# x1 kept in place, a later expert schedule, one program for experts and last stage, and one product moved to GpSimd

## The chip, the cores and the metric

The kernel runs on 1 core of one Trainium2 chip. The metric is the device time of one execution in microseconds, lower is better. Before the change it is 1065.08 us, the median of three runs.

## What is computed

The input is 32 blocks of 256 rows of 128 numbers (8192 rows, fp32). First a recurrent cell runs along each block's rows and its normalised output is added to the input, which gives x1. Then comes a layer with causal attention of 16 heads of 8 dimensions inside each block, a router that picks 2 of 8 experts for each row, the experts (128 to 512 to 128, gelu between), and two more norms.

```python
def reference(x, ...):                       # x: (32, 256, 128)
    x = x + cell(layernorm(x))               # the recurrent cell: x1
    return x + ffn(layernorm(x))

def cell(x):
    i, f, o, z = split(x @ W + b)            # 128 x 512
    i, f = softcap(i + input_bias), -softplus(f)
    # along the rows: m' = max(f + m, i); c = e^(f+m-m') c + e^(i-m') tanh(z); n likewise
    h = sigmoid(o) * c / (n + eps)
    return h / rms(h) * scale

def ffn(x):
    q, k, v = split(x @ w_qkv)               # 16 heads of 8
    o = softmax(causal(q @ k.T / sqrt(8))) @ v
    h = layernorm(x + o @ w_o, g1, b1)
    w = top2(softmax(h @ wg))                # 2 of 8 experts
    moe = sum_e w[e] * (gelu(h @ w1[e] + bb1[e]) @ w2[e] + bb2[e])
    return layernorm(h + moe, g2, b2)
```

## The kernel before

All code is written out engine by engine. Each engine has a function `step(s)` that issues its instructions of that step in a fixed order, and waits on semaphores where it needs another's result. fp32 products that need their precision are made from a high and a low part (`_hi`, `_lo`).

**Cell and attention (0 to about 690 us).** 32 blocks `b` of 256 rows go through a pipeline, one step `s` for each. The cell works in 16 groups `g` of 512 rows, one every second step, some steps ahead of the attention. Its tiles are called `a_...`, those of the attention `b_...`. SP (the queue of SyncE) issues the DMAs of this part, in the order of `step(s)`: in even steps the load of a group of the input into `cell.X` (L491, 256 KB, a ring of NC = 3 groups); the block of x1 into `b_X` (L518, 128 KB); the row of the softmax maxima `b_mt` of block s-3 into row M_ROW = 24 of `c_QK` (L522); the high and low parts of the queries and keys of block s-1 out to DRAM scratch `qk_scr` (L529, L530, L532); in odd steps a group of x1 from `cell.X` to DRAM (L536, 256 KB); a row of zeros into row M_ROW of `c_QK` (L541, 16 KB); and four DMAs that read the queries and keys back from scratch in their new layout into `c_QK` (L547). `c_QK` is a ring of NQ = 3 blocks. Before L541 SP waits until PE has read the block that stood in the buffer. On PE, `maximum(b, u)` makes scores for the row maxima in `b_ps_m`, with a mask product first (L1605 or L1612) and then L1608 or L1615 over all 128 partitions of `c_QK`; since row M_ROW would hold the maxima of an older block there, it is zeroed first. DVE reduces them (L1180), ACT takes the exponentials (L811) of a second set of scores (L1591, L1594) that have the maxima row in them. `rows_stats` (L1340) makes the norm's statistics from `b_X`, `rows_norm` (L852) its normalised rows.

**Experts (about 734 to 997 us).** 71 slots of 256 rows each, sorted by expert, 8 slots to one loop round. PE's order in slot s: twelve products of the up projection (L2028 to L2030) into `e_ps`, the transposes of the rows of slot s+1 (`rows_in`, L2008), the transposes of the output of slot s-1 (`rows_out`, L2015), the eight passes of the down projection of slot s (L2039). ACT applies gelu (L1950) and copies the outcome (L1943), DVE copies the slot's weights (L1965, L1966), makes `e_XW` (L1983), `e_x_lo` (L1970) and `e_Y` (L1991). GpSimd scatters the rows to the DRAM tensor `results` (L1923, two indirect DMAs a slot), first all first choices and then all second choices of the 8192 rows. SP loads `e_X` (L1908, a ring of 8 slots), after the results of the slot 8 back have landed.

**Last stage (about 1002 to 1060 us).** `combine` is a program block of its own, with a barrier of all engines ahead of it. 16 groups of 512 rows: SP loads the two results of each row into `f_G` (L2088, two DMAs of 256 KB a group, ring of four groups), PE adds them into `f_A` (L2131, L2132, ring of three), DVE makes the statistics (L2142, L2148), ACT the root (L2099, L2101), DVE the shift (L2155), ACT the normalised rows `f_Y` (L2115, four a group), DVE multiplies by g2 (L2163) and adds x1 (L2167), ACT's queue stores (L2105).

Of the kernel before, what the change touches and what calls it, by code (L numbers as in the profile page):

```python
# [13 lines left out]
P = 128  # L14
# [92 lines left out]
def cell_memory(nc):  # L107

    cell = Cell()
    with ExitStack() as ctx:  # L110
# [17 lines left out]
        cell.X = sb("a_X", [P, NC, 4, D])  # L128
# [20 lines left out]
        cell.r_rms = sb("a_r_rms", [P, 4])  # L149
    return cell  # L150
# [5 lines left out]
M_ROW = ROWS  # L156
# [3 lines left out]
NB = 5  # L160
NQ = 3
CELL = 12032
NC = 3
NX = 3
# [46 lines left out]
def layers(nc, dram, const, kept):  # L211

    x1_t = dram["x1"].rearrange("(b t p) d -> b p t d", p=P, t=2)
# [6 lines left out]
    with ctx:  # L220
# [21 lines left out]
        zero_row = sb("b_zero", [HEADS, T])  # L242
        X = sb("b_X", [P, NX, 2, D])
# [116 lines left out]
        s_x = [sem(f"b_x{k}") for k in range(NX)]  # L360
# [95 lines left out]

        def stored(engine, g):

            engine.wait_ge(c_out[g % NC], 16 * (g // NC) + 16)

# [15 lines left out]
        WRITES, READS = 3 * 16, 5 * 16  # L476
        BROWS = 2 * E + 4
        FILLED = 3 + 2 * NQ
# [10 lines left out]
        def _(sync):  # L489
# [18 lines left out]
            cell_rows(2)  # L508

            def step(s):  # L510
                if s.base % 2 == 0 and NC <= s.base // 2 + NC < GROUPS:
                    stored(sync, s.base // 2)
                    cell_rows(s.base // 2 + NC)
                if s.exists(B):
                    b, n = s, s.of(NX)
                    need(sync, s_xn, b - (NX - 1))
                    stored(sync, b.base // 2)
                    sync.dma_start(X[:, n], x1_t[bass.ds(b.value(), 1)].rearrange("b p t d -> p (b t) d")).then_inc(s_x[n], 16)  # L518
                if (s - 3).exists(B):
                    b, n = s - 3, (s - 3).of(NQ)  # L520
                    need(sync, s_mtc, b + 1)
                    sync.dma_start(QK[M_ROW:M_ROW + 1, n, 0:NJ].rearrange("o j g n -> o (j g) n").bitcast(fp32), mt[:, :].bitcast(fp32)).then_inc(s_mr[n], 16)  # L522
                if (s - 1).exists(B):

                    b, n = s - 1, (s - 1).of(NQ)
                    need(sync, s_qkhi, b + 1)
                    need(sync, s_qkr[n], b.turn(NQ) * READS)
                    slots = scr[n].rearrange("s p n -> p s n")
                    sync.dma_start(slots[:, 0:4:3], qk_hi[:, :, :].bitcast(fp32)).then_inc(s_qkw[n], 16)  # L529
                    sync.dma_start(slots[:, 1:6:4], qk_hi[:, :, :].bitcast(fp32)).then_inc(s_qkw[n], 16)  # L530
                    need(sync, s_qklo, b + 1)
                    sync.dma_start(slots[:, 2:5:2], qk_lo[:, :, :].bitcast(fp32)).then_inc(s_qkw[n], 16)  # L532
                x = group(s, 4)
                if x.exists(GROUPS):
                    need(sync, c_x1, x + 1)
                    sync.dma_start(out_t[:, 4 * x.base:4 * x.base + 4, :], cell.X[:, x.of(NC)]).then_inc(c_out[x.of(NC)], 16)  # L536
                if (s - 1).exists(B):
                    need(sync, s_s, (b - NQ) * 12 + 12)
                    if b.base < NQ:
                        sync.wait_ge(s_fill, FILLED - 2 * (NQ - 1 - n))  # L540
                    sync.dma_start(QK[M_ROW:M_ROW + 1, n, 0:NJ].rearrange("o j g n -> o (j g) n").bitcast(fp32), zero_row[:, :]).then_inc(s_qkr[n], 16)  # L541
                if (s - 1).exists(B):
                    b, n = s - 1, (s - 1).of(NQ)
                    need(sync, s_qkw[n], b.turn(NQ) * WRITES + WRITES)
                    rows = scr[n].rearrange("(a s) (r j g) n -> j (s r) a (g n)", a=2, g=NG, j=NJ)
                    for j in range(NJ):
                        sync.dma_start(QK[32 * j:32 * j + ROWS, n, j:NJ + 1:NJ - j].rearrange("p a g n -> p a (g n)").bitcast(fp32), rows[j]).then_inc(s_qkr[n], 16)  # L547
# [1689 lines left out]
```

## Times and profile before

| | |
|---|---|
| runs | 1067.49, 1065.08, 1062.44 us |
| profiled execution | 1061.42 us, its span 1059.6 us |
| PE busy | 902.4 us (85%) |
| DVE busy | 849.5 us (80%) |
| ACT busy | 769.8 us (73%) |
| GpSimd busy | 535.0 us (50%) |
| DMA | 114.69 MB, 108 GB/s in the mean |

The span is the time from the first to the last recorded instruction of the profiled execution; 1.8 us of its time lie around it. Times of a row are counted from the span's start. "PE" rows are matmuls, "PEld" their weight loads; "SPq" and "ACTq" are DMA issues by SyncE and ScalarE. A value in square brackets is how long the engine stood idle before the row, and what ended that.

### The profile page before, as it was taken

The numbers are of one execution on the slowest core, as the hardware profiler recorded it, in microseconds if no ns is written. First come the engines' busy times: TensorE is split into PE (matmuls) and PEld (weight loads), VectorE is DVE, ScalarE is ACT, GpSimd is POOL, SyncE is SP. The second block draws the span as 40 slices with busy tenths as digits, with TensorE's granted clock in tenths as the row PEclk, the third lists the DMA queues.
The fourth block names the chain that finished last, engine by engine and source line by source line (L and its number), as shares of the span: only waits on it lengthen the run. The fifth ranks groups of instructions, "written<-read, shape, count | busy, mean of one in ns | idle before, by whom it ended". The sixth has DMA issues, their size and how long they took to land. (4 is left out here: it accounts for less than half of the span.)

```text
span 1059.6 us, 26142 instructions
## 1 busy us (share of the span) xinstructions
PE 902.4 (85%) x6922; PEld 698.3 (66%) x6922; DVE 849.5 (80%) x2533; ACT 769.8 (73%) x1905; POOL 535.0 (50%) x781
## 2 busy tenths in 40 slices
PE   1446899999999999999999998846999999999474
PEld 0234667676766766766676666536999999999421
DVE  4667989999999999998989888673777777777378
ACT  2776799999999999997897766751656656666356
POOL 8000243344356556656577767782555656656400
PEclk9657999999999999998999999965999999999788
DMA  1015543444354454545344556153333332332186
GB/s 52 1 51 130 132 108 108 113 118 111 90 136 118 120 128 118 136 108 124 104 127 126 137 140 160 40 119 102 88 99 86 92 89 85 95 86 67 48 247 190
DMA packets 138118, 114.69 MB, mean 108 GB/s; under 512 B 19459, under 2 KB 126601, under 8 KB 138005
## 3 DMA queue, kind: packets, MB, share of 16 engines
q1 hardware_dynamic: 120916, 92.24, 33.9%
q0 software_dynamic: 8640, 16.93, 5.0%
q10 hardware_dynamic: 8448, 4.20, 1.4%
q8 instruction: 48, 0.79, 0.3%
q14 instruction: 66, 0.53, 0.2%
HBM read 60.60 MB, written 52.58 MB: 107 GB/s over the span
## 5 line engine op out<-in xcount | busy, mean ns | idle before, releaser
L621 POOL TENSOR_SCALAR_AFFINE_SELECT b_PT<-b_PT 128x256 f32<-128x256 f32 (+1 forms) x384 | 191.0, 512 | 207.2 <-ACT b_PT L811 202.1
L1180 DVE TENSOR_REDUCE b_m_neg<-b_ps_m 128x2 f32<-128x512 f32 (+1 forms) x384 | 255.1, 681 | 33.9 <-PE b_ps_m L1615 15.8
L811 ACT ACTIVATE b_PT<-b_ps_s 128x512 f32<-128x512 f32 x384 | 219.6, 598 | 28.3 <-PE b_ps_s L1591 13.9
L1923 POOL DMA_INDIRECT results<-e_Y,e_X x142 | 151.7, 1068 | 121.4 <-DVE e_Y L1991 98.5
L656 POOL DMA_INDIRECT slots<-c_pay,b_pos x128 | 130.3, 1018 | 39.9 <-issue 36.5
L2039 PE MATMUL e_ps_d<-e_h,e_w 128*128 128x256 f32 x568 | 134.5, 380 | 0.0
L1615 PE MATMUL b_ps_m<-c_QK 128*128 128x256 f32 x512 | 123.3, 322 | 0.0
L1594 PE MATMUL b_ps_s<-c_QK 128*128 128x512 f32 x256 | 111.0, 434 | 5.6 <-ACT b_PT L811 5.4
L1950 ACT ACTIVATE e_h<-e_ps,e_w 128x256 f32<-128x256 f32 x284 | 111.3, 480 | 0.8 <-PE e_ps L2030 0.8
L2039 PEld LDWEIGHTS e_ps_d<-e_h,e_w 128*128 128x128 f32 x568 | 102.6, 191 | 11.0
L1943 ACT ACTIVATE e_yt<-e_ps_d,e_w 128x256 f32<-128x256 f32 x71 | 33.7, 475 | 99.2 <-PE e_ps_d L2039 99.2
L1965 DVE CAST e_w<-c_w1s 128x1024 fp32r x71 | 49.4, 696 | 67.6 <-PE e_ps L2030 66.2
L2028 PE MATMUL e_ps<-e_x_hi,e_w 128*128 128x256 f32 x284 | 93.9, 330 | 0.9 <-DVE e_x_lo L1970 0.9
L1608 PE MATMUL b_ps_m<-c_QK 128*128 128x128 f32 x512 | 94.3, 314 | 0.0
L1627 PE MATMUL b_ps_o<-b_PT,b_V 128*32 128x256 f32 x1024 | 82.7, 395 | 1.1 <-POOL b_PT L621 1.1
L1608 PEld LDWEIGHTS b_ps_m<-c_QK 128*128 128x128 f32 x512 | 79.7, 197 | 3.8
L2030 PE MATMUL e_ps<-e_x_hi,e_w 128*128 128x256 f32 x284 | 80.7, 284 | 0.0
L2029 PE MATMUL e_ps<-e_x_lo,e_w 128*128 128x256 f32 x284 | 80.5, 283 | 0.0
L1615 PEld LDWEIGHTS b_ps_m<-c_QK 128*128 128x128 f32 x512 | 79.6, 196 | 0.5
L1612 PE MATMUL b_ps_m<-mask_b,ident_b 128*128 128x256 bf16 x256 | 72.0, 281 | 6.9 <-DVE b_m_neg L1180 6.6
L1605 PE MATMUL b_ps_m<-mask_b,ident_b 128*128 128x512 bf16 x128 | 50.4, 394 | 26.4 <-DMA c_QK<-qk_scr 20.9
L610 POOL TENSOR_TENSOR a_X<-a_Y,a_X 128x512 f32<-128x512 f32 x16 | 20.5, 1281 | 89.1 <-DVE a_Y L1145 89.1
(253 smaller groups left out, 2311.6 us busy)
## 6 DMA issues: line engine op xcount, KB each, us to landing
c_QK<-qk_scr SPq DMA_DIRECT2D x128, 192.0 KB
qk_scr<-b_qk_hi SPq DMA_DIRECT2D x64, 256.0 KB
e_X<-slots SPq DMA_DIRECT2D x71, 130.0 KB, 2.3
qk_scr<-b_qk_lo SPq DMA_DIRECT2D x32, 256.0 KB
f_G<-results SPq DMA_DIRECT2D x32, 256.0 KB, 3.6
a_X<-in_L_attn_x_dram SPq DMA_DIRECT2D x16, 256.0 KB, 6.4
x<-a_X SPq DMA_DIRECT2D x16, 256.0 KB, 2.8
b_X<-x SPq DMA_DIRECT2D x32, 128.0 KB, 5.7
```

Source lines behind the costliest of these rows:

```text
L621: nc.gpsimd.affine_select(out=tri, in_=tri, compare_op=ALU.is_ge, fill=0.0, base=0, pattern=[[0, tri.shape[1]], [1, P]], channel_multiplie ...
L656: nc.gpsimd.indirect_dma_start(dram["slots"][:, :], bass.IndirectOffsetOnAxis(pos[:, q % NPOS, k, i:i + 1], 0), pay[:, r, t, k, :], None). ...
L811: nc.scalar.activation(PT[:, g % 2, q % 3], ps_s[:, q % 2], ACT.Exp, scale=HD ** -0.5).then_inc(s_e, 1)
L1180: nc.vector.tensor_reduce(out, scores, AX.X, ALU.max, negate=True).then_inc(s_red, 1)
L1594: nc.tensor.matmul(ps_s[:, q % 2].rearrange("p (j q) -> p j q", j=2), QK[:, n, NJ, g, 0:P], QK[:, n, 2 * u - 2:2 * u, g, :], start=True, s ...
L1608: done = nc.tensor.matmul(ps_m[:, u % 2, j * P:(j + 1) * P], QK[:, n, j, u, 0:P], QK[:, n, NJ, u, 0:P], start=False, stop=(j == 3), skip_g ...
L1615: done = nc.tensor.matmul(ps_m[:, u % 2, j * T:(j + 1) * T], QK[:, n, 2 * jp + j, g, P:T], QK[:, n, NJ, g, :], start=False, stop=(j == 1), ...
L1627: nc.tensor.matmul(ps_o[32 * j:32 * j + VW, g // 2, :], v_block(n, 0, g, j), PT[:, g % 2, 1 + j // 2, (j % 2) * T:(j % 2 + 1) * T], start= ...
L1923: nc.gpsimd.indirect_dma_start(dram["results"][:, :], bass.IndirectOffsetOnAxis(X[:, j.of(NB_X), u, D:D + 1].bitcast(u32), 0), Y[:, n, u, ...
L1950: nc.scalar.activation(h1[:, n, c], ps_1[:, c, 0:SUB * P], ACT.Gelu_apprx_tanh, bias=w2[:, n, F + c:F + c + 1]).then_inc(s_g, 1)
L2028: nc.tensor.matmul(out, w1[:, n, 1, col], x_hi[:, n], start=True, stop=False)
L2039: last = nc.tensor.matmul(ps_d[:, 0:SUB * P], w2[:, n, c * D:(c + 1) * D], h1[:, n, c], start=(c == 0), stop=(c == NF - 1))
```

## The change

1. The tile `b_X` and its 32 loads are gone. `rows_stats` and `rows_norm` read block b out of `cell.X`, where the cell has left x1. The ring of `cell.X` grows from 3 to 6 groups. The next group is loaded by `recurrent_in` at the end of an even step, when the group six back has been stored and the rows of its second block have been normalised. The load used to stand at the head of an even step, directly behind the reads of the odd step.
2. The maxima row moves from partition 24 to partition 127, and the products for the maxima read partitions 0 to 119 only (KEYS = 120). The row of zeros is no longer written. The wait that stood before it stands before the reads.
3. The results of one row lie side by side in DRAM, and the 64 rows of one partition (row p*64 and after) too: `dest` gives p*128 + 2t + k for row t of partition p and choice k. The last stage loads a group in one DMA of 512 KB with 4 KB pieces, where it took two of 256 KB with pieces of 512 bytes.
4. Experts: in step s PE now does the up projection of s, `rows_in` of s+2, `rows_out` of s-2, and the down projection of s-1. Up projections of even and odd slots go to different halves of `ps_1`, w2 has four buffers in place of two. ACT and DVE follow (`yt` and `Y` of s-2, halves of s+2).
5. `combine` gives back functions that the experts' block calls at its end; there is no block of its own and no barrier between. `f_A` is `ps_1`. SP waits for the last results by itself, PE for the last gelu.
6. The product with g2 goes from DVE (L2163) to GpSimd.

```diff
-NC = 3
-NX = 3
+NC = 6
+KEYS = 32 * (NJ - 1) + ROWS
-M_ROW = ROWS
+M_ROW = 127
+            def recurrent_in(s):
+                g = s.base // 2 - 1 + NC
+                if s.base % 2 or not NC <= g < GROUPS:
+                    return
+                stored(sync, g - NC)
+                need(sync, s_xn, Count(2 * (g - NC) + 2))
+                cell_rows(g)
...
+            def operands(b):
...
+                need(sync, s_qkw[n], b.turn(NQ) * WRITES + WRITES)
+                need(sync, s_s, (b - NQ) * 12 + 12)
...
+                for j in range(NJ):
+                    sync.dma_start(QK[32 * j:32 * j + ROWS, n, j:NJ + 1:NJ - j]..., rows[j]).then_inc(s_qkr[n], 16)
...
             def step(s):
-                if s.base % 2 == 0 and NC <= s.base // 2 + NC < GROUPS:
-                    stored(sync, s.base // 2)
-                    cell_rows(s.base // 2 + NC)
-                if s.exists(B):
-                    b, n = s, s.of(NX)
-                    need(sync, s_xn, b - (NX - 1))
-                    stored(sync, b.base // 2)
-                    sync.dma_start(X[:, n], x1_t[...]).then_inc(s_x[n], 16)
...
-                    sync.dma_start(QK[M_ROW:M_ROW + 1, n, 0:NJ]..., zero_row[:, :]).then_inc(s_qkr[n], 16)
+                a, b1, x = s - 1, s - 3, group(s, 4)
+                maxima_row(b1)
+                columns_high(a)
+                columns_low(a)
+                recurrent_out(x)
+                operands(a)
+                recurrent_in(s)
...
             for s in range(GROUND, STEPS_B):
                 step(Count(s))
+                if s == B - 2:
+                    stored(sync, GROUPS - 1)
...
-                nc.gpsimd.iota(dest[:, :, :], pattern=[[P, NTILE], [B * T, TOPK]], base=0, channel_multiplier=1)
+                nc.gpsimd.iota(dest[:, :, :], pattern=[[TOPK, NTILE], [1, TOPK]], base=0, channel_multiplier=TOPK * NTILE)
...
             def rows_stats(n):
-                need(dve, s_x[k], n.turn(NX) * 16 + 16)
+                need(dve, c_x1, Count(n.base // 2 + 1))
                 need(dve, s_mv, n)
                 for t in range(2):
-                    last = nc.vector.bn_stats(stats[:, t, :], X[:, k, t, :])
+                    last = nc.vector.bn_stats(stats[:, t, :], cell_row(n, t))
...
-                        done = nc.tensor.matmul(ps_m[...], QK[:, n, j, u, 0:P], QK[:, n, NJ, u, 0:P], ...)
+                        done = nc.tensor.matmul(ps_m[...], QK[0:KEYS, n, j, u, 0:P], QK[0:KEYS, n, NJ, u, 0:P], ...)
...
+    r_t = dram["results"].rearrange("(p t k) d -> p t k d", p=P, k=TOPK)
+    def on_sync(sync):
+        for sem_of, count in landed:
+            sync.wait_ge(sem_of, count)
+        for g in range(GROUPS):
...
+            sync.dma_start(G[:, n], r_t[:, 4 * g:4 * g + 4]).then_inc(s_g[n], 16)
...
+    def on_gpsimd(pool):
+        for g in range(GROUPS):
+            m = g % 2
+            pool.wait_ge(s_y0, 4 * g + 4)
+            if g >= 2:
+                pool.wait_ge(s_y3, g - 1)
+            nc.gpsimd.tensor_tensor(Y1[:, m], Y0[:, m], kept["g_b"][:, :, :].to_broadcast([P, 4, D]), ALU.mult).then_inc(s_y1, 1)
...
+        def summed(g):
+            dve.wait_ge(s_y1, g + 1)
...
+            nc.vector.tensor_tensor(Y3[:, g % 3], Y1[:, m], kept["x1"][:, 4 * g:4 * g + 4, :], ALU.add).then_inc(s_y3, 1)
...
             def step(s):                      # PE, experts
...
+                        if c % 2 == 0:
+                            need(pe, s_g, (s - 2) * NF + (c + 2))
...
-                if (s + 1).exists(SLOTS):
-                    rows_in(s + 1)
-                if (s - 1).exists(SLOTS):
-                    rows_out(s - 1)
-                if s.exists(SLOTS):
-                    need(pe, s_yt, s)
+                if (s + 2).exists(SLOTS):
+                    rows_in(s + 2)
+                if (s - 2).exists(SLOTS):
+                    rows_out(s - 2)
+                j = s - 1
+                if j.exists(SLOTS):
+                    need(pe, s_yt, j)
```

The order of the DMAs on SP in an odd step of the pipeline and in the even step behind it, before (lines without an x count are one DMA):

```order
L532 DMA qk_scr<-b_qk_lo 128x2x256
L536 DMA x1<-a_X 128x4x128
L541 DMA c_QK<-b_zero 1x16x256
L547 DMA c_QK<-qk_scr 24x2x1024 x4
L491 DMA a_X<-in_L0_attn_x_dram 128x4x128
L518 DMA b_X<-x1 128x2x128
L522 DMA c_QK<-b_mt 1x16x256
L529 DMA qk_scr<-b_qk_hi 128x2x256
L530 DMA qk_scr<-b_qk_hi 128x2x256
L532 DMA qk_scr<-b_qk_lo 128x2x256
L541 DMA c_QK<-b_zero 1x16x256
L547 DMA c_QK<-qk_scr 24x2x1024 x4
```

and the same stretch now, with the line numbers of the changed kernel:

```order
L544 DMA qk_scr<-b_qk_lo 128x2x256
L550 DMA x1<-a_X 128x4x128
L562 DMA c_QK<-qk_scr 24x2x1024 x4
L525 DMA c_QK<-b_mt 1x16x256
L534 DMA qk_scr<-b_qk_hi 128x2x256
L535 DMA qk_scr<-b_qk_hi 128x2x256
L544 DMA qk_scr<-b_qk_lo 128x2x256
L562 DMA c_QK<-qk_scr 24x2x1024 x4
L491 DMA a_X<-in_L0_attn_x_dram 128x4x128
```

The loads of `a_X` and `b_X` no longer follow the reads of the odd step; that of `a_X` now follows the reads of the even step, and that of `b_X` and the zero row are gone.

PE at the end of the experts, after the last product of the last up projection, before:

```order
L2030 MATMUL e_ps_1<-e_x_hi,e_w1 128x256
L2015 MATMUL e_ps_y<-ident,e_yt 128x128 x2
L2039 MATMUL e_ps_d<-e_h1,e_w2 128x256 x4
L2015 MATMUL e_ps_y<-ident,e_yt 128x128 x2
L1855 UNCONDITIONAL_BRANCH
L2124 UNCONDITIONAL_BRANCH
L2131 MATMUL f_A<-f_G,ident 128x512
```

and now:

```order
L2203 MATMUL e_ps_1<-e_x_hi,e_w1 128x256
L2186 MATMUL e_ps_y<-ident,e_yt 128x128 x2
L2213 MATMUL e_ps_d<-e_h1,e_w2 128x256 x4
L2186 MATMUL e_ps_y<-ident,e_yt 128x128 x2
L2213 MATMUL e_ps_d<-e_h1,e_w2 128x256 x4
L2186 MATMUL e_ps_y<-ident,e_yt 128x128 x2
L1961 MATMUL e_ps_1<-f_G,ident 128x512
```

One more down projection and one more pair of transposes stand behind the last up projection, and the branches to another program are gone.

DVE in two groups of the last stage, before:

```order
L2155 SCALAR_TENSOR_TENSOR f_shift<-f_mv,f_rstd 128x4
L2142 BN_STATS f_st<-f_A 128x6 x4
L2148 BN_AGGR f_mv<-f_st 128x2 x4
L2163 TENSOR_TENSOR f_Y1<-f_Y0,c_g 128x512
L2167 TENSOR_TENSOR f_Y3<-f_Y1,c_x1 128x512
```

and now, where GpSimd has sixteen rows of the product behind its last scatter:

```order
L1984 SCALAR_TENSOR_TENSOR f_shift<-f_mv,f_rstd 128x4
L1971 BN_STATS f_st<-e_ps_1 128x6 x4
L1977 BN_AGGR f_mv<-f_st 128x2 x4
L1992 TENSOR_TENSOR f_Y3<-f_Y1,c_x1 128x512
```

DVE's add now waits for GpSimd, and the next group's statistics stand behind it in the same queue.

## Rows read from the trace of the kernel before

**Rows 1.** Windows: stretch, length, busy of PE PEld DVE ACT POOL, clock, DMA share, GB/s.

```profile
300.00:400.00 100.00, 94.01 (x827) 68.72 (x829) 96.51 (x265) 93.04 (x222) 58.85 (x97) 1.00 0.48 120
...
600.00:690.00 90.00, 80.52 (x762) 55.22 (x761) 70.86 (x230) 61.15 (x149) 64.75 (x115) 0.98 0.44 116
```

**Rows 2.** Waits in 80 to 690 us: engine, line, releaser, total us, times, longest.

```profile
PE b_ps_m L1605 <- DMA c_QK<-qk_scr: 20.9, 18, 3.7
...
SPq L541 <- PE b_ps_s L1594: 63.4, 29, 3.4
...
SPq L547 <- DMA qk_scr<-b_qk_lo: 4.9, 7, 1.7
```

**Rows 3.** Timeline of PE, a block's first product: four of the eighteen waits.

```profile
88.25 0.61 PE L1605 MATMUL b_ps_m<-mask_b,ident_b 128*128 128x512 bf16 x1 [3.74 <-DMA c_QK<-qk_scr]
...
105.70 0.39 PE L1605 MATMUL b_ps_m<-mask_b,ident_b 128*128 128x512 bf16 x1 [1.07 <-DMA c_QK<-qk_scr]
...
341.72 0.39 PE L1605 MATMUL b_ps_m<-mask_b,ident_b 128*128 128x512 bf16 x1 [0.94 <-DMA c_QK<-qk_scr]
...
493.26 0.54 PE L1605 MATMUL b_ps_m<-mask_b,ident_b 128*128 128x512 bf16 x1 [2.09 <-DMA c_QK<-qk_scr]
```

**Rows 4.** Timeline of SP's queue: an early even step, then odd and even step.

```profile
98.66 1.55 SPq L547 DMA_DIRECT2D c_QK<-qk_scr  x4
...
332.78 0.51 SPq L541 DMA_DIRECT2D c_QK<-b_zero  x1
333.66 1.56 SPq L547 DMA_DIRECT2D c_QK<-qk_scr  x4
335.26 0.39 SPq L491 DMA_DIRECT2D a_X<-in_L_attn_x_dram  x1
335.76 0.45 SPq L518 DMA_DIRECT2D b_X<-x  x1
...
351.38 2.10 SPq L547 DMA_DIRECT2D c_QK<-qk_scr  x4
```

**Rows 5.** Window behind the longest wait of the middle.

```profile
494.00:504.00 10.00, 9.79 (x62) 7.03 (x62) 6.23 (x17) 5.78 (x12) 4.24 (x7) 0.69 0.30 96
```

**Rows 6.** Windows: a hundred us of the experts; early in the last stage.

```profile
800.00:900.00 100.00, 100.00 (x669) 94.22 (x668) 73.83 (x224) 61.01 (x168) 59.53 (x57) 1.00 0.32 90
1010.00:1030.00 20.00, 14.63 (x30) 5.27 (x29) 16.64 (x77) 11.90 (x38) 0.00 (x0) 0.95 0.81 232
```

**Rows 7.** Timeline in the experts: a second scatter, then SP's next load.

```profile
861.36 1.03 POOL L1923 DMA_INDIRECT results<-e_Y,e_X  x1 [0.30 <-issue]
...
863.87 0.40 SPq L1908 DMA_DIRECT2D e_X<-slots  x1
```

**Rows 8.** DMA issues of the page: median us from issue to landing.

```profile
slots<-c_pay,b_pos POOLq DMA_INDIRECT x128, 3.4
```

**Rows 9.** Timeline, from the last slot to the last stage's first product.

```profile
992.82 0.44 PE L2015 MATMUL e_ps_y<-ident,e_yt 128*128 128x128 f32 x2 [0.56 <-ACT e_yt L1943]
...
996.08 0.98 POOL L1923 DMA_INDIRECT results<-e_Y,e_X  x1 [0.30 <-issue]
...
1006.24 2.08 PE L2131 MATMUL f_A<-f_G,ident 128*128 128x512 f32 x2 [12.98 <-DMA f_G<-results]
```

**Rows 10.** Chain that ended last: its first load, two turns of its loop.

```profile
1001.62 0.37 SPq L2088
...
1021.74 1.10 PE f_A L2131 x2
1022.83 0.87 PE f_A L2132 x2
...
1027.15 1.10 PE f_A L2131 x2
```

**Rows 11.** One 128x512 product on GpSimd and on DVE, ns min/median/max.

```profile
L610 POOL TENSOR_TENSOR a_X<-a_Y,a_X x16: 1267/1282/1294, 57.0 to 596.1; 128x512 f32<-128x512 f32 x16
...
L2163 DVE TENSOR_TENSOR f_Y<-f_Y,c_g x16: 655/658/693, 1016.2 to 1055.5; 128x512 f32<-128x512 f32 x16
```

More of the change, by code:

```diff
@@ L149, in cell_memory @@
         cell.r_rms = sb("a_r_rms", [P, 4])
+        cell.X = sb("a_X", [P, NC, 4, D])
     return cell
@@ L161 @@
 NQ = 3
-CELL = 12032
-NC = 3
-NX = 3
+CELL = 13056
+NC = 6
 NV = 4
@@ new lines, in _, with maxima_row @@
+            for g in range(3, NC):
+                cell_rows(g)
[5 more added lines that the diff above has]
+                need(sync, s_xn, Count(2 * (g - NC) + 2))
+                cell_rows(g)
+            def maxima_row(b):
+                if not b.exists(B):
+                    return
+                n = b.of(NQ)
+                need(sync, s_mtc, b + 1)
+                sync.dma_start(QK[M_ROW:M_ROW + 1, n, 0:NJ].rearrange("o j g n -> o (j g) n").bitcast(fp32), mt[:, :].bitcast(fp32)).then_inc(s_mr[n], 16)
@@ new lines, in columns_high, with columns_low @@
+            def columns_high(b):
+                if not b.exists(B):
+                    return
+                n = b.of(NQ)
+                need(sync, s_qkhi, b + 1)
+                need(sync, s_qkr[n], b.turn(NQ) * READS)
+                slots = scr[n].rearrange("s p n -> p s n")
+                sync.dma_start(slots[:, 0:4:3], qk_hi[:, :, :].bitcast(fp32)).then_inc(s_qkw[n], 16)
+                sync.dma_start(slots[:, 1:6:4], qk_hi[:, :, :].bitcast(fp32)).then_inc(s_qkw[n], 16)
+            def columns_low(b):
+                if not b.exists(B):
+                    return
+                n = b.of(NQ)
+                need(sync, s_qklo, b + 1)
+                need(sync, s_qkr[n], b.turn(NQ) * READS)
+                slots = scr[n].rearrange("s p n -> p s n")
+                sync.dma_start(slots[:, 2:5:2], qk_lo[:, :, :].bitcast(fp32)).then_inc(s_qkw[n], 16)
@@ L1890, in run_experts @@
         s_go = sem("e_go")
+        last_stage = combine(nc, ctx, dram, const, kept, ps_1,
+                             [(s_out[k], 32 * len(range(k, SLOTS, NB_E))) for k in range(NB_E)], (s_g, SLOTS * NF))
         block = ctx.enter_context(nc.Block())
@@ L1996, in step @@
                     nc.vector.tensor_tensor(row, row, kept["b_b"][:, :, :], ALU.add).then_inc(s_xb, 1)
-            steps(dve, SLOTS, 1, NB_X, step, 8)
+            steps(dve, SLOTS, 2, NB_X, step, 8)
             dve.wait_ge(s_xb, NTILE)
+            last_stage["vector"](dve)
         @block.tensor
@@ L2179, in constants @@
+            steps(pe, SLOTS, 2, NB_X, step, 8)
+            last_stage["tensor"](pe)
 def constants(nc, ctx, dram):
```

339 lines of the change are left out of this document (154 added, 185 removed).

## The prediction

> **What bounds the kernel now.** I read the windows of busy time first, then the table of waits, then the timeline of SP's queue, and the chain of work for the end.
>
> In the pipeline (80 to 690 us) two engines are nearly full: in the middle window PE is busy 94.0 and DVE 96.5 of 100 us [rows 1]. Only in 600 to 690 is DVE free a fifth of the time (70.9 of 90). PE's own greatest wait is for the queries and keys, 20.9 us in 18 waits at the first product of a block [rows 2]. In the middle they come every second step, .2 to 1.2 us each, ten of them 8.8 us in sum with the one of 2.09; the first three (3.74, 1.07, 1.62) make 6.4 and the last five 5.7; four of the eighteen are shown [rows 3]. SP's queue says why every second one: behind the four reads of an odd step stand at once the loads of `a_X` and `b_X`, 384 KB, and those reads need 341.72 - 333.66 = 8.1 us until PE may start. The early even step, with `b_X` alone behind, needs 105.70 - 98.66 = 7.0 [rows 3, 4]. Ahead of the reads the zero row takes .51, and its wait for PE is a long one in 29 of 32 steps [rows 2, 4].
>
> In the experts PE is busy 100.00 of 100 us [rows 6]; nothing but PE's own work counts there, 3.6 us a slot. Between the last slot and the last stage lie a landing, the end of a program and a first load [rows 9, 10]. The last stage is a loop of 1027.15 - 1021.74 = 5.41 us for two groups: PE's sums, DVE's statistics, ACT's root and rows. L2163 isn't in it [rows 10].
>
> **The reads of queries and keys (parts 1 and 2).** Two things bring them earlier. Without the zero row SP issues them up to .55 sooner; where the writes to scratch land last (7 waits of L547 [rows 2]; at 333.66 a gap of .37 [rows 4]) it is nothing, so 0 to .55. With nothing behind them in an odd step they take at most the 7.0 of the step that had `b_X` behind, 1.0 less. Together 1.0 to 1.6, against waits of .2 to 1.2. Of the ten middle waits all but a rest of the 2.09 go: 8 us of PE time. DVE has the same work as before, at 96% busy, and part of the time won waits for it, so I count half: **-4**. At the start the first and third reads have nothing behind them and the second now has `a_X`: about 3 of 6.4 us go, -2.5. At the end DVE isn't full and counts whole, but the last three reads have weight loads behind them that stay; the first two of the five (.8 each) go, and up to .5 from each of the other three where the writes let them: -2. Sum **-8.5**. Bounds: -2 if DVE alone sets the middle; -20 if all 20.9 goes.
>
> In the even steps the load of `a_X` now stands where `b_X` did, 128 KB more. By the 8.1 above the reads come 1.1 later, less the zero row's .55. No even step of the middle shows a wait: the timeline has all ten of them behind an odd step's reads, so there is some room over the 7.0. I take it that it holds .5 and count nothing; if it doesn't, up to .5 in each of 12 even steps (+6). The statistics read `cell.X` itself, so their rows are there a store and a load earlier; the ring of six groups gives the loads twelve steps. One wait for the last store is new, at a point where it was issued a whole step before; behind it stand only weight loads. Partitions 0 to 119 in place of 128 change no count of columns: nothing.
>
> **Experts (part 4).** PE issues the same instructions in a slot and never waits, so a slot stays 3.6 us: 0 in 71 slots. The first up projection now stands behind the transposes of two slots' rows: +.2, a guess. At the end one down projection and one pair of transposes follow that before ran under an up projection: work is only moved, but the stall of .56 at L2015 [rows 9] comes twice and the outcome's last rows one turn later, +.8. Sum **+1**, bounds 0 and +2.5. SP loads slot s+8 2.5 us behind the scatter [rows 7], or 3.4 by the page's row for the other scatter [rows 8]. PE now wants the rows a slot earlier and gives results a slot later; of some 13 us of slack 6 stay.
>
> **One program (part 5).** The last scatter starts at 996.08, so its rows land at 998.6 to 999.5; the first load is issued at 1001.62 [rows 9, 10]. SP now waits for the landing itself: 2.1 to 3.0 go, **-2.6**. If other engines' ends had cost nothing it would be 0. Without the second issue (.37) -.4. The first sum on PE takes 2.08 at a lowered clock where a later one takes 1.10 [rows 9, 10]; PE stands idle there as before, so I count no gain.
>
> **The product on GpSimd (part 6).** Its like on GpSimd takes 1.28 us, on DVE .66 [rows 11]. DVE's busy time falls by 16 x .66 = 10.5, but it isn't in the loop. What is: the add of group g waits for the product, and shift and the statistics of group g+3 stand behind it. From ACT's last row of group g: product 1.28 with handovers .15, add .69, shift .16, so 2.3 us; PE's sum of g+3 is there after .14 + 1.10 + .87 = 2.1 [rows 10] and DVE began .18 behind that. The statistics begin .1 later, eight turns: +.6, bounds 0 and +3. At the very end the product stands open: 1.28 - .66 = +.65. Sum **+1.25**.
>
> The Trainium skill, GPSIMD Engine Reference, section Engine selection, puts elementwise work with two inputs on VectorE, GpSimd being about 2 times slower. The rows agree (1.95 times) [rows 11]. By that rule alone the edit would cost 16 x .62 = 10 us; by the chain most of it is covered.
>
> **Results in one piece (part 3).** The last stage needs 512 KB each 2.7 us, 190 GB/s, and moved 232 GB/s with its stores [rows 6]; PE waits for a load only at the start. So larger pieces bring nothing in the loop; the first load perhaps some tenths, not counted. The price is what the new layout may do: the 128 partitions of a load now start 64 KB apart in DRAM, where they were 512 bytes apart. No row shows such a load: 0 is taken.
>
> The Trainium skill, DMA: Bandwidth & Descriptors, section Latency and other measured facts, says that loads whose partitions lie a large power of two apart slow down, from 207 GB/s at 512 KiB to 103 at 4 MiB. It gives no figure for 64 KB, and no run here shows one.
>
> **Sum.** -8.5 + 1 - 2.6 - .4 + 1.25 = -9.25. The profiled execution took 1061.42 us, so 1052.2. That execution lay 3.7 below the median of the runs, 1065.08; on that scale **1055.8**.
>
> **Rivals.** *DVE bounds the pipeline.* PE's waits go and come back as waits for DVE at L1612 or L1605; the middle gives nothing, start and end 2: -2 and -.75 from the rest, 1062.3. For it: 96.5 of 100 in the window [rows 1]. Against it: the waits stand at a block's start, and DVE then waits for PE too (15.5 us at L1608 [rows 2]). That the reads take 8 us for a reason other than the loads behind them ends at the same time. Chance .22.
>
> *All waits count, and the clock with them.* Behind the wait of 2.09 the granted clock is .69 for 10 us, the lower level of 1.2 GHz for much of that stretch [rows 5]; a third of full speed missing for 10 us is 3 us of PE's work. With that and all 20.9 less the rests of the last steps the pipeline gives -20 in place of -8.5: 1044. Chance .12.
>
> *Slower: loads at 64 KB distance.* If a load of 512 KB takes over 2.7 us of the whole DMA capacity, the last stage is bound by it. At half of the 232 GB/s [rows 6] a group takes 512 / 116 = 4.5 us besides its share of stores, 1.8 more in 16 groups: +29, so 1085. It decides from 512 KB in 3.6 us (16 x .9 = 14.6 eats up 9.25 and 5.3 more). Against it: a row's 4 KB are in one piece. Chance .05. The same end from GpSimd, if its product with a broadcast operand took over 3 us: eight turns x 1.8; chance .03.
>
> **Chances.** Forecast .58, DVE .22, clock .12, slower .08. A measurement of this kernel can tell about .5%, 5.3 us, from no change; so faster is below 1059.8. The forecast's own range is 1050 to 1060.5, nine tenths of it faster; with the clock and a little of the first rival that makes .70 faster, .21 the same, .09 slower. Range 1045 to 1067: it takes in the DVE rival and half of the clock's.
>
> **What would show it.** Waits of L1605 for `c_QK` under 8 us in sum, reads of odd steps landing in about 7 us, those of even steps in 8. If DVE bounds, PE's waits for L1180 grow by as much. Experts: 3.6 us a slot, PE without a wait. The first `f_G` load within .1 of the last landing, about 2 us before the end of the experts used to allow. The loop of the last stage at 5.5 us. I am wrong if even steps begin to wait for `c_QK`, if the slot isn't 3.6, if PE waits for `f_G` in the loop, or if products and adds of the last stage take turns.

## The result and the profile after

The changed kernel takes 1051.62 us, the median of four runs (1049.19 to 1057.74), against 1065.63 us, the median of four, before. The ratio is 0.989, with a 95% interval of 0.984 to 0.993: 1.1% faster. The profiled execution took 1051.34 us, its span is 1049.6 us, 10.1 us shorter than that of before.

Where the 10.1 us come from can be read by laying marks at the same events of both traces (each time is a row's start; the pipeline ends at the last mask product of shape 128x512).

| stretch | before | after | difference | forecast |
|---|---|---|---|---|
| start to end of pipeline | 664.93 | 656.58 | -8.35 | -8.5 |
| to the first transposes of the experts | 69.16 | 69.06 | -0.1 | 0 |
| to the first up projection | 1.61 | 2.16 | +0.55 | +0.2 |
| to the last up projection | 254.32 | 252.57 | -1.75 | with the next line |
| to the last scatter | 6.06 | 9.20 | +3.15 | +0.8 for the two |
| to the first load of results | 5.54 | 2.25 | -3.3 | -2.6 |
| to the first sum on PE | 4.61 | 4.25 | -0.4 | -0.4 |
| to the first statistics | 3.82 | 3.86 | 0 | 0 |
| to the end | 49.59 | 49.62 | 0 | +1.25 |

**The reads.** In SP's queue of the changed kernel, the stretch that answers to [rows 4], an odd step has nothing behind its reads, and `a_X` stands behind those of the even step:

```profile
332.14 1.56 SPq L562 DMA_DIRECT2D c_QK<-qk_scr  x4
...
349.24 1.55 SPq L562 DMA_DIRECT2D c_QK<-qk_scr  x4
350.89 0.39 SPq L491 DMA_DIRECT2D a_X<-in_L_attn_x_dram  x1
```

PE's waits for `c_QK` between 80 and 690 us fell from 20.9 us in 18 waits [rows 2] to 8.2 in 5. What became of them shows in a stretch of the middle, 142 to 440 us. PE's waits there, first in the kernel before:

```profile
PE b_ps_m L1605 <- DMA c_QK<-qk_scr: 6.5, 8, 1.2
PE b_ps_s L1594 <- ACT b_PT L811: 2.4, 8, 0.3
PE b_ps_m L1605 <- DVE b_m_neg L1180: 2.3, 3, 0.8
```

and in the changed kernel:

```profile
PE a_ps_r L1540 <- DVE a_xt_lo L1074: 4.8, 8, 0.7
PE b_ps_s L1618 <- ACT b_PT L836: 2.3, 8, 0.3
PE b_ps_m L1632 <- DVE b_m_neg L1205: 2.3, 3, 0.8
```

Eight waits for the queries, one every second step, are gone; eight waits for DVE's low part of the cell's rows (L1074) stand in their place, and PE's other waits are as they were. 6.5 us were removed and 4.8 came back elsewhere. That leaves 1.7. Two even steps, in which `a_X` is now loaded behind the reads, wait longer than before: block 1's first product 1.50 us in place of 1.07, and block 29's 1.92 in place of 0.82.

**The clock.** The middle alone can't make 8.35. Two windows of the kernel before, and the same two of the changed kernel (columns as in [rows 1]):

```profile
490.00:500.00 10.00, 7.91 (x31) 5.53 (x30) 7.31 (x19) 5.43 (x11) 7.97 (x13) 0.67 0.35 81
520.00:530.00 10.00, 8.66 (x76) 5.74 (x74) 9.75 (x40) 7.94 (x21) 5.61 (x10) 0.87 0.37 116
```

```profile
490.00:500.00 10.00, 9.58 (x92) 7.24 (x92) 9.83 (x33) 8.34 (x20) 7.56 (x13) 1.00 0.37 113
520.00:530.00 10.00, 8.93 (x90) 5.98 (x91) 9.97 (x30) 8.56 (x21) 7.38 (x12) 1.00 0.58 145
```

The granted clock was 0.67 and 0.87 in these windows before and is 1.00 now. Over 490 to 535 us it was 0.89, so 0.11 x 45 = 5.0 us of full speed were missing. Between the maxima rows of blocks 20 and 24 (SP's 16 KB DMA of `b_mt`, a mark of each block) lie 82.2 us before and 77.1 after: 5.05 of the 8.35 us come in these four blocks. The wait of 2.09 us that went stands there too, and this pair alone doesn't part the two.

**The experts.** PE is as full as it was [rows 6]:

```profile
800.00:900.00 100.00, 100.00 (x670) 94.25 (x668) 74.72 (x223) 64.10 (x168) 63.69 (x56) 1.00 0.32 89
```

**The end.** Timeline of the changed kernel from the drain of the experts to the first sum, against [rows 9]:

```profile
983.17 0.44 PE L2186 MATMUL e_ps_y<-ident,e_yt 128*128 128x128 f32 x2 [0.56 <-ACT e_yt L2109]
983.45 1.89 PE L2213 MATMUL e_ps_d<-e_h,e_w 128*128 128x256 f32 x8
...
985.90 0.44 PE L2186 MATMUL e_ps_y<-ident,e_yt 128*128 128x128 f32 x2 [0.56 <-ACT e_yt L2109]
...
989.57 0.98 POOL L2085 DMA_INDIRECT results<-e_Y,e_X  x1 [0.30 <-issue]
991.82 10.40 SPq L1911 DMA_DIRECT2D f_G<-results  x6
996.07 2.05 PE L1961 MATMUL e_ps<-f_G,ident 128*128 128x512 f32 x2 [9.73 <-DMA f_G<-results]
```

The stall of 0.56 stands there twice, as forecast. The first load follows the start of the last scatter by 2.25 us, where it was 5.54. The first product still takes 2.05 us for two: PE had been idle for 9.73 and the granted clock is 0.50 from 996 to 1000 us, as it was before at that point.

In the last stage the waits of the changed kernel read:

```profile
DVE f_Y L1992 <- POOL f_Y L1952: 10.9, 12, 1.7
PE e_ps L1961 <- ACT f_Y L1937: 10.5, 11, 1.7
```

DVE now waits 10.9 us for GpSimd's product, about what its saved 16 x 0.66 = 10.5 us come to, and PE waits for ACT as long as before (10.6 us).

### The profile page after: what moved, and what is told of

Same layout as the page of the kernel before. It is cut to its first block and busy times, and to the rows that moved or that the text cites. A ratio compares the mean times of both kernels' runs of the same rounds, so it can differ in the third digit from the quotient of the medians.

```text
span 1049.6 us, 26096 instructions
## 1 busy us (share of the span) xinstructions
PE 899.5 (86%) x6884; PEld 697.8 (66%) x6922; DVE 842.1 (80%) x2517; ACT 775.1 (74%) x1905; POOL 560.8 (53%) x796
## 5 line engine op out<-in xcount | busy, mean ns | idle before, releaser
L2085 POOL DMA_INDIRECT results<-e_Y,e_X x142 | 158.4, 1116 | 116.6 <-DVE e_Y L2161 92.8
L681 POOL DMA_INDIRECT slots<-c_pay,b_pos x128 | 130.2, 1018 | 40.4 <-issue 38.6
L1639 PE MATMUL b_ps_m<-c_QK 120*128 120x256 f32 x512 | 123.5, 323 | 0.0
L1632 PE MATMUL b_ps_m<-c_QK 120*128 120x128 f32 x512 | 94.5, 314 | 12.7 <-DMA c_QK<-qk_scr 8.2
L1651 PE MATMUL b_ps_o<-b_PT,b_V 128*32 128x256 f32 x1024 | 82.2, 393 | 1.1 <-POOL b_PT L646 1.1
L1632 PEld LDWEIGHTS b_ps_m<-c_QK 120*128 120x128 f32 x512 | 79.8, 197 | 3.9
L1639 PEld LDWEIGHTS b_ps_m<-c_QK 120*128 120x128 f32 x512 | 79.5, 195 | 0.5
L2139 DVE TENSOR_TENSOR e_x_lo<-e_ps_t,e_x_hi 128x256 fp32r<-128x256 f32 x71 | 30.1, 424 | 40.5 <-ACT e_x_hi L2099 40.5
```

The source lines that it names most:

```text
L681: nc.gpsimd.indirect_dma_start(dram["slots"][:, :], bass.IndirectOffsetOnAxis(pos[:, q % NPOS, k, i:i + 1], 0), pay[:, r, t, k, :], None). ...
L1632: done = nc.tensor.matmul(ps_m[:, u % 2, j * P:(j + 1) * P], QK[0:KEYS, n, j, u, 0:P], QK[0:KEYS, n, NJ, u, 0:P], start=False, stop=(j == ...
L1639: done = nc.tensor.matmul(ps_m[:, u % 2, j * T:(j + 1) * T], QK[0:KEYS, n, 2 * jp + j, g, P:T], QK[0:KEYS, n, NJ, g, :], start=False, stop ...
L1651: nc.tensor.matmul(ps_o[32 * j:32 * j + VW, g // 2, :], v_block(n, 0, g, j), PT[:, g % 2, 1 + j // 2, (j % 2) * T:(j % 2 + 1) * T], start= ...
L2085: nc.gpsimd.indirect_dma_start(dram["results"][:, :], bass.IndirectOffsetOnAxis(X[:, j.of(NB_X), u, D:D + 1].bitcast(u32), 0), Y[:, n, u, ...
```

## The experiments

The experiments ran on other chips than the two kernels above, and there all kernels are slower: the kernel before takes 1084.5 us in the first group and about 1096 us in the others, where single executions of it lie anywhere between 1075 and 1107 us. So a kernel is compared with the kernel before on its own chip, and stage by stage with the others. One mark is steady over all chips: the time from the maxima row of block 2 to that of block 18.

**The changed kernel again.** No edit.

> The changed kernel once more, to see how far stages move from execution to execution. Both theories: within 4 us of 1051.6, the last block's first mask product within 2 us of 656.6, c_QK waits of PE 7 to 10 us.

Measured: 1073.7 us against 1084.5 (median of 10 and 13 runs), ratio 0.991 (0.987 to 0.995). The change is worth the same on this chip. The pipeline ended at 669.2, not 656.6: this chip is slower from about block 20 on. c_QK waits 5.1 us.

**The loads of b_X back.**

```diff
+                block_rows(s)
                 maxima_row(b1)
...
-                need(dve, c_x1, Count(n.base // 2 + 1))
+                need(dve, s_x[n.of(NX)], n.turn(NX) * 16 + 16)
...
```

`block_rows` waits for the store of x1 and loads the block into `b_X`, 128 KB; statistics and normalised rows read it from there.

> The changed kernel with the tile b_X and its 32 loads of 128 KB back where they stood (at the head of each step, behind the reads), all else as changed. Forecast's theory (what stands behind the reads delays them, PE's waits count half while DVE is near full): reads of odd steps 0.3 to 0.7 us longer, those of even steps to 8 us or more; c_QK waits from 8 to about 13 us, the pipeline's end 2 to 3 us later, total +2 to +4 us. DVE theory (DVE bounds the pipeline): the waits return, the end moves by under 1 us. Full theory: the end moves by all of the added waits, +5 us.

Measured: 1071.75 us, ratio 0.989 (0.980 to 0.997). No c_QK wait in 142 to 440 us; 6.9 us in all.

**The load of a_X behind the odd reads.**

```diff
+                recurrent_in(s - 2)
                 maxima_row(b1)
...
                 operands(a)
-                recurrent_in(s)
```

> The changed kernel with the 256 KB load of a_X moved back from behind the reads of even steps to directly behind those of odd steps. Forecast's theory: odd reads 0.7 to 1 us longer; in the middle waits of up to 0.5 us in some of ten steps, c_QK waits +2 to +4 us, the pipeline's end +1 to +2 us. DVE theory: waits back, end under +0.5 us. If the load behind the reads isn't what delays them: no wait comes back.

Measured: 1073.85 us, ratio 0.990 (0.982 to 0.997). c_QK waits 6.9 us in all, 0.5 in 142 to 440.

**The zero row back.**

```diff
-                need(sync, s_qkw[n], b.turn(NQ) * WRITES + WRITES)
                 need(sync, s_s, (b - NQ) * 12 + 12)
...
+                sync.dma_start(QK[M_ROW:M_ROW + 1, n, 0:NJ]..., zero_row[:, :]).then_inc(s_qkr[n], 16)
+                need(sync, s_qkw[n], b.turn(NQ) * WRITES + WRITES)
```

> The changed kernel with the row of zeros (16 KB, one DMA, 0.51 us of SP) written again ahead of the reads in each step. Forecast's theory: reads issued 0.55 us later in most steps, c_QK waits +1 to +2 us (start and end of the pipeline), end of pipeline +1 to +2 us. DVE theory: under +0.5 us. Full theory: +0.5 in each of some twenty steps whose wait for the queries sets the pace, +8 us or more.

Measured: 1071.9 us, ratio 0.988 (0.980 to 0.995). c_QK waits 9.4 us in all, 0.5 in 142 to 440.

So none of the three shows in the time by itself, and each brings back less waiting than expected. The three together:

**All three back.** The edits of the last three in one kernel; products over 120 rows and the ring of six stay.

> The changed kernel with all three back that were put back singly: the zero row, the loads of b_X, and the load of a_X directly behind the reads of odd steps. Singly none moved the time. Forecast's theory, that the room over the reads is used up only by the sum: c_QK waits of 15 to 21 us, the pipeline's end +5 to +8 us against the changed kernel. DVE theory: waits 15 to 21 us, end within 2 us. Then the gain of the pipeline would lie in what stays changed here: the products over 120 rows, the rows read in place or the ring of six.

Measured: 1079.7 us, ratio 0.990 (0.982 to 0.997). c_QK waits 17.8 us in all. PE's wait in 142 to 440 us of this kernel, with none left for `a_xt_lo`:

```profile
PE b_ps_m L1647 <- DMA c_QK<-qk_scr: 7.2, 8, 1.3
```

and of the kernel that has only the zero row back:

```profile
PE a_ps_r L1543 <- DVE a_xt_lo L1077: 3.6, 8, 0.6
PE b_ps_m L1632 <- DMA c_QK<-qk_scr: 0.5, 2, 0.3
```

The waits of the middle return only in the sum: each of the three by itself fits into the room that the other two leave. Two of them together weren't tried. And they return in place of the waits for DVE.

**The halves of the change.** The kernel before once more, parts 1 and 2 alone, and parts 3 to 6 alone. The two halves are whole functions taken from one kernel or the other; the only line in the wrong half is the table of result rows:

```diff
-                nc.gpsimd.iota(dest[:, :, :], pattern=[[P, NTILE], [B * T, TOPK]], base=0, channel_multiplier=1)
+                nc.gpsimd.iota(dest[:, :, :], pattern=[[TOPK, NTILE], [1, TOPK]], base=0, channel_multiplier=TOPK * NTILE)
```

> The kernel before once more, for its stages on the chip that the experiments use: its own time, ratio 1. Both theories: c_QK waits of PE near 20.9 us, the last block's first mask product 7 to 10 us later than in the changed kernel on the same chip.

> Parts 1 and 2 alone (cell and attention of the changed kernel, experts, last stage and layout of results as before). Forecast: -8.5 us against the kernel before, ratio 0.992. DVE theory: -2 us, 0.998. Full theory: -15 us or more, 0.986.

> Parts 3 to 6 alone (cell and attention as before, experts, one program, layout and product of the changed kernel). Forecast: +1 -2.6 -0.4 +1.25 = -0.75 us against the kernel before; by the stages of the two first traces -1.7 us. If parts 3 to 6 carry the gain and the reads none: -8 us or more.

Measured, beside runs of the kernel before at 1096.4 us: the kernel before 1096.3 us, ratio 1.003 (0.993 to 1.012); parts 1 and 2 alone 1090.65, ratio 1.002 (0.997 to 1.007); parts 3 to 6 alone 1077.7, ratio 0.986 (0.978 to 0.995). These are medians of executions that scatter widely. Their means are 1092.6 us for the kernel before, 1092.0 for parts 1 and 2, and 1079.6 for parts 3 to 6. On this chip the half that was to bring 8.5 us brings nothing that can be told, and the half that was to bring 0.75 brings about 15 (1.4% of 1096, with an interval from 0.5% to 2.2%).

For the pipeline the steady mark gives the size. From block 2 to block 18 the four profiled kernels with the reads of before take 297.2, 297.0, 298.3 and 297.5 us (the kernel before on two chips, parts 3 to 6 alone, all three back). The ten others, with all or some of the new reads, take 295.4 to 295.7. The 298.3 holds a drop of the clock (0.83 in 305 to 315 us, behind a wait of 1.58 us for the queries); the three others lie 1.7 us above the ten, and that agrees with the two tables of waits, 6.5 less 4.8. It is about a quarter of what the waits came to and under half of the forecast. The kernel with all three back has the products over 120 rows and the ring of six and takes 297.5 us, so those two bring nothing here.

What differs by more is the granted clock, and it goes with the waits. Here are PE's first product of block 2 and the window behind it, of the kernel with a_X behind the odd reads, and of the changed kernel on the same chip:

```profile
119.28 0.39 PE L1629 MATMUL b_ps_m<-mask_b,ident_b 128*128 128x512 bf16 x1 [1.66 <-DMA c_QK<-qk_scr]
120.00:130.00 10.00, 10.00 (x55) 6.89 (x55) 5.92 (x14) 5.95 (x12) 1.45 (x3) 0.66 0.24 81
```

```profile
118.93 0.39 PE L1629 MATMUL b_ps_m<-mask_b,ident_b 128*128 128x512 bf16 x1 [0.81 <-DMA c_QK<-qk_scr]
120.00:130.00 10.00, 10.00 (x84) 7.53 (x84) 9.30 (x25) 9.29 (x20) 3.21 (x6) 1.00 0.37 112
```

Block 2's maxima row came 3.4 us later in the first (143.94 and 140.56), and the distance was still 3.4 at block 18 (439.61 and 436.24). One such drop costs more than all steady waits of sixteen blocks.

It follows the edits. In five of the profiled kernels `a_X` is loaded directly behind the reads of block 2. They wait 1.62 to 2.15 us there, and the four with 1.66 or more have a lowered clock in 120 to 130 us (0.66 or 0.83). The nine others wait 0.63 to 1.41 us and have 1.00 in that window. Where `a_X` stands behind the reads of block 1, four of the nine have a drop one block earlier, in 105 to 112 us, with waits of 1.20 to 1.62 us there; the five others waited 0.45 to 1.44 us and have none. The maxima row of block 2 comes at 141.9 to 145.1 us in the five, 143.5 in the mean, and at 140.3 to 143.4 in the nine, 141.3 in the mean.

For the experts the windows of parts 1 and 2 alone (the old schedule) and of parts 3 to 6 alone (the new one), on one chip:

```profile
840.00:860.00 20.00, 18.20 (x113) 15.38 (x112) 12.51 (x38) 11.31 (x30) 10.75 (x10) 1.00 0.29 81
900.00:940.00 40.00, 36.87 (x235) 32.15 (x236) 25.98 (x78) 23.30 (x60) 21.37 (x19) 1.00 0.27 77
```

```profile
840.00:860.00 20.00, 20.00 (x135) 18.76 (x133) 15.60 (x47) 13.17 (x36) 13.53 (x12) 1.00 0.34 95
900.00:940.00 40.00, 40.00 (x270) 37.73 (x269) 29.52 (x89) 25.77 (x67) 25.07 (x22) 1.00 0.32 91
```

PE isn't full under the old schedule here, in 18.20 of 20 and 36.87 of 40 us. From slot 19 to slot 66 nearly every second slot takes 3.9 to 5.1 us in place of 3.6, and from the first to the last up projection it is 280.3 us against 257.2. On the first chip the old schedule had no such slot.

**One slot of lag in the changed kernel.** `run_experts` of before, with the calls of the last stage: the order of the steps, w2 in two buffers, the up projections in one set of buffers and ACT's waits for them come back together. PE's part of the edit:

```diff
-                if (s + 2).exists(SLOTS):
-                    rows_in(s + 2)
-                if (s - 2).exists(SLOTS):
-                    rows_out(s - 2)
-                j = s - 1
+                if (s + 1).exists(SLOTS):
+                    rows_in(s + 1)
+                if (s - 1).exists(SLOTS):
+                    rows_out(s - 1)
...
-                if j.exists(SLOTS):
-                    need(pe, s_yt, j)
+                if s.exists(SLOTS):
+                    need(pe, s_yt, s)
```

> The changed kernel with the experts' schedule of before (one slot of lag in place of two, w2 in two buffers); reads, one program, layout and product as changed. Forecast, from the first traces: a slot stays 3.60 us on PE with either schedule, experts -0.5 to -1 us by the shorter drain, total -1. Lag theory, from the chip of the last four runs, where the schedule of before took 276 and 280 us between the first and the last up projection and that of two slots 253 and 257: every second slot of the schedule with one slot of lag takes up to 1.4 us more from about slot 19 on, experts +15 to +25 us, total ratio near 1.00 against the kernel before, unless the chip is like the first one.

Measured: 1094.7 us, ratio 0.998 (0.989 to 1.008). No gain is left that can be told. First to last up projection 276.5 us; up to the last scatter 6.06 us against 10.0 to 10.9 in most kernels with two slots of lag on these chips (12.2 in one). The two-slot kernels on this chip took 256.2 to 257.2 us from the first to the last up projection. So in these traces the schedule is worth about 20 us less 4 for its drain, 16 us. Whole executions say it less sharply: the twelve with two slots of lag on this chip lie between 1074.6 and 1087.4 us, the 23 with one slot (this kernel and the kernel before) between 1078.0 and 1105.1. The schedule hardly shortens the best executions; it keeps the long ones away. How a slow slot comes about, from the timelines of ACT and PE of this kernel:

```profile
855.16 0.47 ACT L2112 ACTIVATE e_h<-e_ps,e_w 128x256 f32<-128x256 f32 x1 [1.77 <-remote]
...
855.69 0.70 PE L2203 MATMUL e_ps_d<-e_h,e_w 128*128 128x256 f32 x2 [0.90 <-ACT e_h L2112]
```

ACT stands still for 1.77 us before its last gelu, at the end of something that isn't an engine or a DMA of this core ("remote"), and the down projection of the same slot waits for that gelu 0.90 us. With two slots of lag the down projection takes the gelu of the slot before, finished a slot earlier. Neither kernel of the first pair has such a stall of ACT. With two slots of lag on these chips ACT's stalls in 760 to 980 us come to 3.7 us in the changed kernel and 5.2 in parts 3 to 6 alone, and PE is full in the windows above. With one slot they come to 16.2 us in 15 stalls here and 18.1 and 17.8 in the two other profiled kernels. So it isn't only that PE no longer waits for a stalled gelu: the stalls themselves are nearly gone. Which of the parts that come back here brings them, and how, these runs don't show.

**A program block of its own.**

```diff
-        block = ctx.enter_context(nc.Block())
+        own = ExitStack()
+        block = own.enter_context(nc.Block())
...
-            last_stage["sync"](sync)
...
+        own.close()
+        with nc.Block() as block:
+            for name in ("sync", "gpsimd", "scalar", "vector", "tensor"):
+                getattr(block, name)(last_stage[name])
```

The calls of the last stage go from the four other engines too.

> The changed kernel with the last stage in a program block of its own again, barrier ahead of it. Forecast: first load of results 5.5 us behind the last scatter's start in place of 2.25, so +3.3 us and nothing else. Rival (engines' ends cost nothing): 0.

Measured: 1083.0 us, ratio 0.990 (0.981 to 0.998). Its last scatter and its first load:

```profile
1019.23 0.98 POOL L2085 DMA_INDIRECT results<-e_Y,e_X  x1 [0.30 <-issue]
1024.87 1.77 SPq L1911 DMA_DIRECT2D f_G<-results  x4
```

5.64 us, against 2.25 in the changed kernel on both of its chips: +3.4, as expected.

**The product on DVE.**

```diff
     def on_gpsimd(pool):
-        for g in range(GROUPS):
...
-            nc.gpsimd.tensor_tensor(Y1[:, m], Y0[:, m], ..., ALU.mult).then_inc(s_y1, 1)
+        pass
...
         def summed(g):
             m = g % 2
+            dve.wait_ge(s_y0, 4 * g + 4)
...
+            nc.vector.tensor_tensor(Y1[:, m], Y0[:, m], ..., ALU.mult).then_inc(s_y1, 1)
```

> The changed kernel with the product with g2 on DVE as before. Forecast: from the first statistics to the end 1.25 us less (0.6 in the loop, 0.65 at the end). DVE-bound reading of the last stage: +5 to +10 us. By the first two traces (49.55 before, 49.67 after): -0.1.

Measured: 1080.1 us, ratio 0.988 (0.981 to 0.996). From the first statistics to the end 49.35 us, against 50.3 to 50.8 in the three others on this chip. Split at the last group's statistics it is clearer. From those to the end the four kernels with the product on DVE take 8.1 to 8.3 us and the ten with it on GpSimd 9.2 or 9.3, on all four chips: 0.9 to 1.1 us, for a forecast 0.65. The loop ahead of that takes 41.2 us here and 41.1 to 41.5 in the three others, so nothing of the forecast 0.6 shows on this chip; on the chip of the halves it is 40.6 and 40.9 with DVE, 41.3 and 41.7 with GpSimd. In the first pair the loop was 0.9 us shorter with GpSimd (41.3 and 40.4), which hid the price at the end. Why it was shorter there stays open.

**The results in two halves.**

```diff
-    r_t = dram["results"].rearrange("(p t k) d -> p t k d", p=P, k=TOPK)
+    r_t = dram["results"].rearrange("(k t p) d -> p k t d", p=P, k=TOPK)
...
-            sync.dma_start(G[:, n], r_t[:, 4 * g:4 * g + 4]).then_inc(s_g[n], 16)
+            for k in range(TOPK):
+                sync.dma_start(G[:, n, k], r_t[:, k, 4 * g:4 * g + 4, :]).then_inc(s_g[n], 16)
```

> The changed kernel with the results of first and second choices in two halves again, two loads of 256 KB with pieces of 512 bytes a group. Forecast: first load to first sum +0.4 us, last stage and experts unchanged otherwise, total +0.4. Theory that the distance of 64 KB costs: last stage shorter by 1 us or more. Theory that small pieces cost: PE waits for f_G in the loop, last stage +2 us or more.

Measured: 1081.0 us, ratio 0.987 (0.979 to 0.995). First load to first sum 4.00 us (3.8 to 4.4 in the others with the changed layout), first statistics to the end 50.31 (50.6 and 50.8 in the two others of this chip with the product on GpSimd), first to last up projection 257.2 (256.2 and 257.1). The layout is worth nothing that shows here, either way.

None of these beats the changed kernel clearly. The product back on DVE would save about 1 us, which these runs can't tell from the spread.

## Why the prediction was right, and where it wasn't

The time was forecast at 1055.8, with 1045 to 1067; it is 1051.6. In the profiled execution -9.25 was forecast and -10.1 measured. The reads and the single program carry that, and that the reads' sum came so near is in part luck: 5 of their 8.35 us lie where the clock had dropped before, and the forecast had no such term.

**The reads: total right, terms wrong.** Forecast -2.5 at the start, -4 in the middle, -2 at the end. By the block marks the first pair has -0.5 up to block 2, -1.5 to block 18, -0.3 to block 20, -5.05 in blocks 20 to 24 and -1.0 behind. The failed step is "so I count half": of the 6.5 us of waits between blocks 2 and 18 some 1.7 count, a quarter. I took DVE's 96% as a reason to halve. The trace of before had more to say, which I didn't follow: with the queries earlier, PE's next need in the same step is the low part of the cell's rows from DVE, and PE waits for that up to 0.7 us every second step. The DVE rival gave the middle nothing; the truth lies between, nearer to it.

Its full price of 1062 didn't come, since the clock gave back up to 5 us, which I had kept for the third rival. That the drop of the clock went with the wait of 2.09 [rows 3, 5] fits what the experiments show at block 2: drops stand behind PE's longer waits. It isn't the whole rule: the kernel with all three back waited 1.35 us at the same place as the wait of 2.09 and kept a clock of 1.00, and on the other chips drops stand behind waits of about 2 us for ACT as well (in the kernels with a block of its own and with the results in two halves, at 498 us). So such a gain is real where it falls, but its size changes from execution to execution: over blocks 20 to 24, the 5.05 us of the first pair, the changed kernel took 80.2 us on another chip and the kernel before 81.1 on a third.

The start was forecast at -2.5 and gave -0.5 in the first pair. Over all profiled kernels, sorted by where `a_X` is loaded, it is -2.2 at block 2, so there the first pair was the exception. The reads behave as the prediction says: with nothing behind them PE may start 6.7 and 6.8 us after the issue (blocks 0 and 2), with `a_X` behind them 7.5 (block 1). But PE still waits 2.87, 1.50 and 1.11 us in these blocks, 5.5 us in place of 6.4: about 1 us of waiting went, not 3.

On the chip of the halves the reads alone gave a ratio of 1.002. The pipeline ends at 674.9 to 681.0 us in the three profiled kernels of that chip with the old reads, and at 669.2 to 679.0 in the eight of all three chips with the new ones (two of them with the loads of `b_X` or the zero row back; the one with only `a_X` behind the odd reads ends at 674.7). The means are 677.3 and 672.4. The difference of 5 us is of the size of the scatter.

That each of the edits counts 0.5 to 1 us of delay in the middle was also too simple. One back brings at most 0.5 us of waits between 142 and 440 us, three back bring 7.2.

**The experts: right on the first chip, mis-sized elsewhere.** "A slot stays 3.6 us" holds for both kernels of the first pair. The drain was mis-sized: +0.8 was forecast, and it is +3.15 from the last up projection to the last scatter, of which 1.75 only moves a down projection behind that mark; net +1.4, and +0.55 at the start for +0.2. What I left out altogether is what a slot of slack does when an engine stalls. No stall was in the trace of before, so its price was set at 0; in the traces of two other chips it is 16 us, more than all the rest. How the added slot comes to keep the stalls away stays open.

**One program: right in mechanism, a little over its bounds.** -2.6 was forecast between 2.1 and 3.0; 3.3 and 3.4 were measured. SP issues the first load 2.25 us behind the start of the last scatter, so the rows have landed by then. The landing of 2.5 was the better of my two bounds, and 3.4, taken from another scatter, was too long.

**The product: right in mechanism.** DVE waits for it and the loop hides it; nothing in sum on the first chip, 1.0 to 1.5 us on the chip where it was moved back, 1.25 forecast. The end costs 0.9 to 1.1 for .65. The loop's +.6 doesn't follow from its own figures: the product's path is put at 2.3 us and the old one at 2.1 + .18, so nothing was left to count, and on the chip where the product was moved back nothing shows. DVE's 10.5 us of work saved bought nothing. The Trainium skill, GPSIMD Engine Reference, section Engine selection, which keeps such work on VectorE, gives the right direction but by itself the wrong size (10 us).

**The layout: right at 0.** With the results in two halves nothing changes. The slower rival, loads at 64 KB distance, is refuted by that run and by PE's waits in the last stage, which name ACT and not the loads. The figures that the prediction takes from the Trainium skill, DMA: Bandwidth & Descriptors, section Latency and other measured facts, are of copies of 16 KiB a partition between tensors in DRAM, not of loads of 4 KB pieces.

## What to carry to other kernels

A wait on a nearly full engine is worth what is left when the next wait of the same step ends: before booking it, look in the trace for what that engine needs next and when it is ready. A wait can cost more than its length, since the clock may drop behind it: a block came 3.4 us later here where PE had waited 1.66 us in place of 0.81. Edits that all work on one delay belong together in an experiment, since each alone may sit inside the room that the others leave. And a schedule with a slot more of slack can be worth nothing on one chip and about 1% on the next, so a trace without stalls doesn't price it.

## What the runs showed of the hardware that I had not expected

Between chips the same kernel differs by up to 3% in the median (the kernel before: 1065.6, 1084.5, 1095.2 and 1096.4 us) and by 1.2 to 1.5% in its fastest execution (1062.4, 1077.8, 1078.0 and 1075.1). The difference isn't spread evenly: up to block 20 the same kernel agrees within 2 us on all chips. Behind it, on the slower chips only, engines stand still for up to 4.2 us at a time, ended by what the profile calls remote: 12 such stalls of ACT with 25.3 us in the changed kernel's profile, 31 with 40.5 in that of parts 1 and 2 alone, none in either trace of the first chip. What they are these runs don't show; no run changed the length of the code or of the loop.

A wait of PE that is 0.8 us longer, 1.66 in place of 0.81, stood ahead of a window with a granted clock of 0.66 in place of 1.00, and all that followed came 3.4 us later. PE was busy 10.00 of 10 us in both windows, so the column of busy time doesn't show the drop; the clock's does.
